# Full attention of 16 narrow heads with maxima made in advance: the last five units cut into two of 256 queries each, in place of the last one only

## The reference, cut to what matters

```
q = _rope(proj(Wq, bq)); k = _rope(proj(Wk, bk)); v = proj(Wv, bv)
scores = jnp.einsum('bhqd,bhkd->bhqk', q, k) / jnp.sqrt(HEAD_DIM)
attn = jax.nn.softmax(scores, axis=-1)
ctx = jnp.einsum('bhqk,bhkd->bhqd', attn, v)
...
scores = jnp.einsum('bhqd,bhkd->bhqk', q, k) / np.float32(np.sqrt(hd))
scores = scores * scale[..., None]
aw = jax.nn.softmax(scores, axis=-1)
out = jnp.einsum('bhqk,bhkd->bhqd', aw, v).transpose(0, 2, 1, 3).reshape(b, s, d)
```

## Time and profile before

| | before |
|---|---|
| time, median of 3 runs | 3846.15 us (3838.41 to 3847.82) |
| time of the profiled execution | 3843.74 us |
| span of the profiled execution | 3841.9 us |
| PE busy | 3509.3 us, 91% of the span |
| DVE busy | 3039.8 us, 79% |
| ACT busy | 2333.1 us, 61% |
| POOL busy | 155.4 us, 4% |
| score products of maxima, line 1987 | 3712, mean 398 ns |
| maxima on DVE, line 2095 | 3456, 2108.3 us |
| exponentials, line 2053 | 1856, 1854.7 us |
| value products, line 2029 | 13824, mean 384 ns |
| granted TensorE clock, mean | 0.928 |

### The profile page before, as it was taken

One profiled execution on the slowest core, in us unless ns is written; L12 is line 12 of the kernel. 1 busy time (PEld: TensorE's weight loads), 2 busy tenths in 40 slices (PEclk: granted clock), 3 DMA queues, 4 the chain that ended last, 5 costly groups with the idle time before them and its releaser, 6 DMA issues.

```text
span 3841.9 us, 72549 instructions
## 1 busy us (share of the span) xinstructions
PE 3509.3 (91%) x29391; PEld 1433.7 (37%) x29391; DVE 3039.8 (79%) x6567; ACT 2333.1 (61%) x2742; POOL 155.4 (4%) x417
## 2 busy tenths in 40 slices
PE   5989899889999997899999989599997999999988
PEld 3766766612222224222222245222224222222264
DVE  5255755689999974899999837698974999999557
ACT  2222342238888884388888852257784488888832
POOL 0000000110000000100000000200001000000000
PEclk8889999969999998699999989689998799999989
DMA  0010210130000001300000000400002100000000
GB/s 29 1 45 1 53 32 1 29 99 21 2 2 2 2 2 33 99 2 2 2 2 2 2 23 1 121 2 2 2 2 73 50 2 2 2 2 2 3 22 12
DMA packets 32116, 75.94 MB, mean 20 GB/s; under 512 B 10370, under 2 KB 25542, under 8 KB 26406
## 3 DMA queue, kind: packets, MB, share of 16 engines
q1 hardware_dynamic: 31638, 69.64, 6.3%
q10 hardware_dynamic: 144, 1.66, 0.1%
HBM read 56.54 MB, written 14.73 MB: 19 GB/s over the span
## 4 chain that ended last, share of the span: by engine, by line
PE 48%; DVE 43%; ACT 4%; issue 2%; SPq 2%; POOL 1%; DMA 1%; ACTq 0%; DVEq 0%
DVE pm L2095 36%; PE ps L2029 9%; PE ps L1987 6%; PE ps L966 4%; PE ps L2010 3%; PE ps L969 3%; PE ps L2311 3%; PE ps L1046 3%; PE ps L2332 2%; ACT arena L2053 2%; PE ps L1269 2%; SPq L1406 1%; PE ps L765 1%; PE ps L2026 1%; PE ps L1646 1%
## 5 line engine op out<-in xcount | busy, mean ns | idle before, releaser
L2095 DVE TENSOR_REDUCE pm<-ps 128x1 f32<-128x512 f32 x3456 | 2108.3, 680 | 92.6 <-PE ps L1987 87.1
L2053 ACT ACTIVATE arena<-ps 128x1024 f32<-128x1024 f32 (+1 forms) x1856 | 1854.7, 1001 | 438.1 <-PE ps L2010 310.0
L1987 PE MATMUL ps<-arena 64*128 64x512 bf16 (+1 forms) x3712 | 1303.3, 398 | 55.8 <-DMA arena<-parts_dram 43.2
L2029 PE MATMUL ps<-arena,VA 128*16 128x256 f32 (+1 forms) x13824 | 1079.7, 384 | 29.1 <-ACT EV L2074 24.2
L2010 PE MATMUL ps<-arena 64*128 64x512 bf16 (+1 forms) x3520 | 1017.0, 379 | 8.7 <-DMA arena<-m_dram 8.0
L1987 PEld LDWEIGHTS ps<-arena 64*128 64x128 bf16 x3712 | 329.6, 93 | 1110.3 <-DVE pm L2095 859.1
L2029 PEld LDWEIGHTS ps<-arena,VA 128*16 128x16 f32 x13824 | 228.1, 94 | 505.9 <-ACT arena L2053 400.0
L2010 PEld LDWEIGHTS ps<-arena 64*128 64x128 bf16 x3520 | 186.5, 94 | 64.3 <-issue 49.0
L985 ACT ACTIVATE EV<-ps 128x512 f32<-128x512 f32 x128 | 76.3, 598 | 203.3 <-PE ps L966 203.3
L997 DVE TENSOR_TENSOR arena<-EV,ps 128x512 f32<-128x512 f32 x128 | 87.7, 685 | 120.9 <-PE ps L969 115.4
L966 PE MATMUL ps<-XNT,arena 128*128 128x512 f32 x304 | 161.4, 613 | 2.3 <-DVE arena L1325 1.5
(11 more groups left out here) (280 smaller groups left out, 2831.0 us busy)
## 6 DMA issues: line engine op xcount, KB each, us to landing
arena<-parts_dram SPq DMA_DIRECT2D x192, 128.0 KB, 2.9
parts_dram<-parts SPq DMA_DIRECT2D x32, 384.0 KB, 2.9
arena<-in_pad SPq DMA_DIRECT2D x16, 512.0 KB, 7.6
arena<-k_dram SPq DMA_DIRECT2D x20, 268.0 KB, 4.2
arena<-in_w SPq DMA_DIRECT2D x4, 1024.0 KB, 5.8
parts<-k_dram SPq DMA_DIRECT2D x8, 268.0 KB, 3.9
arena<-in_w12T SPq DMA_DIRECT2D x1, 2048.0 KB, 9.5
arena<-m_dram SPq DMA_DIRECT2D x122, 6.0 KB
```

Of the source, the lines that this page charges most:

```text
L1987: ins = e.matmul(bank[:, 0:w], QR[half(par), q, 2 * g + pp, qt * P:(qt + 1) * P], KT[half(par), kc, 2 * g + pp, 0:w], start=True, stop=True)
L2029: ins = e.matmul(c.bank(4)[32 * hh:32 * hh + VW, a:b], c.VA[:, j, GH * g + hh, :], self.PB[:, (first + hh) % self.PBS, a:b], start=j == 0 ...
L2053: e.activation(self.PB[:, s:s + 2, offs[0]:CH], c.bank(t % 4, 2).rearrange("p (a t) -> p a t", a=2)[:, :, offs[0]:CH], ACT.Exp, scale=self ...
L2095: e.tensor_reduce(top, bank, AX, ALU.max).then_inc(self.emptied_v.sem, 1)
```

## The change: five units cut in two

The class gets a constant HALVED = 5, and in a full stage the last five units (11 to 15), not the last one alone, are replaced by two each, of the first and of the last 256 queries. They are called 11a, 11b and so on here. The units of the causal stage stay as they are.

```
-    LEAD, EARLY, AHEAD = 9, 4, 14
+    LEAD, EARLY, AHEAD, HALVED = 9, 4, 14, 5
...
         else:
-            g, k, _, _ = self.units.pop()
-            self.units += [(g, k, 0, TPC // 2), (g, k, TPC // 2, TPC)]
+            last = self.units[-self.HALVED:]
+            self.units[-self.HALVED:] = [(g, k, a, a + TPC // 2) for g, k, _, _ in last for a in (0, TPC // 2)]
```

## The result

The change makes the kernel slower, by less than half of what was forecast:

| | before | after |
|---|---|---|
| time, median of 10 runs | 3845.89 us (3838.41 to 3851.34) | 3854.01 us (3848.41 to 3856.86) |
| ratio, 95% interval | | 1.0020 (1.0012 to 1.0028) |
| span of the profiled execution | 3841.9 us | 3851.8 us |
| DVE busy | 3039.8 us | 3048.2 us |
| PE busy | 3509.3 us | 3514.4 us |

What follows compares the result with a forecast made beforehand. VectorE's reductions bound the kernel, with TensorE just fitting under; after the change both bind. Three full stages at +7.0 us give +21 us on the profiled 3843.74, 3864.7; forecast 3865 us, range 3851 to 3884.

Steps and rivals of the forecast that it cites:

- step 1: Score products in ticks of two maxima: four narrow ones idle half of TensorE's rows, +0.11 us, a tick of 1.20 us.
- step 3: TensorE's sum over half units in a full stage: both engines bind, 0.9 us per half unit, 7.0 us a stage.
- step 2: More unit ends on VectorE: four added joins, "rows" and outputs raise its floor by 3.4 us a stage (2.5 to 4.0).
- The low bound: In ticks of two maxima: the third score product overtakes the second, so narrow products add 0 us; dropped for program order.
- Step 3's low end: Lowest total for a full stage with both engines at their bound: 4.8 us, in a range to 10.2.
- The price of a matmul by itself: Two more score products a tick on TensorE: 25 ns each by the skill's page, put at nothing.
- Step 4: GpSimd's 5 operations and SyncE's 3 DMAs for each added unit, and ScalarE's 8 more tile copies, cost nothing.
- Rival A: TensorE doesn't bind in two-maxima ticks; only VectorE's floor is left: +10 us, 3854 (3851 to 3856); chance 0.26.
- Rival B: Narrow score products cost more than columns: ticks of 1.31 us, 3899, or 3882 with half of that; chance 0.10.
- Rival C: Stretches behind the second and third full stage run at TensorE's full clock: 22 us saved, 3832, faster; chance 0.03.

## Why the prediction was wrong

The direction and the bound were right: VectorE's reductions set the pace at 0.598 us each, and a full stage pays for each added unit end. What was wrong is the size: 7.0 us a stage were forecast and 2.5 measured. Of the 4.5 too much, 3.6 come from step 1 and what step 3 built on it, and 0.9 from step 2.

- **Step 1, "if the third, on the free half, can't overtake it, that half idles"; I took +0.11 us a tick. It failed.** It can. The trace of the change shows the second maximum starting before a score product that is ahead of it, the tick with narrow products alone is 1.09 us as before, and the reversed parities cost nothing. I said that rows of before couldn't tell, which is so, and chose the middle by the rule of the Trainium skill, TensorE: Matmul & The Clock Gate, on what overlaps with packed tiles (matmuls start and end in program order). This trace disagrees with it: 1303.51 before 1303.61. The low bound should not have fallen away on it, when the rows showed that products wait but not in which order they start.
- **Step 3, "both are at their bound in every tick", fell with it.** Where TensorE catches up, its ticks stayed at 1.09 to 1.18 us, so it kept the slack with which it works off copies and transposes. VectorE got no gaps: between 1217 and 1400 us it waited 0.6 us in all for products of line 1987, and 1.2 us before the change. The 0.9 us a half unit was 0.31 (20.01 - 19.70).
- **Step 2, VectorE's floor, was the right sum, mis-sized.** I had +3.4 us a stage, measured +2.5. Join and "rows" are 0.52 together, not 0.62, since I took the output step from the starts of its two instructions (0.51) and it costs 0.62 to 0.64. A half-width one is 0.37, put at 0.4, so that splitting an output step adds 0.12 and three add under 0.4, where 0.9 was taken.
- **Step 3's low end**, 4.8 us a stage, doesn't follow from its terms, which give 6.5 x 0.7 + 0.6 + 0.5 = 5.65.
- **The price of a matmul by itself** was put at nothing, and the ticks of 1.09 us with two more products bear that out. The Trainium skill, TensorEngine Tiling (Array Packing), on instruction overhead, has about 60 cycles for each; this trace doesn't show them as an addition.
- **Step 4 was right.** The chains by GpSimd and SyncE, four more a stage, cost no more than this: the half units keep 20.01 us to a hundredth.
- **Rival A** was the case, by its mechanism (overtaking) and nearly by its time: 3854 stood there and 3854.01 was measured. That the numbers meet to 0.01 us is luck: it added 10 us to an execution 2.15 us under the median, and the rise was 8.1. I gave it 0.26. **Rival B** is out by the narrow products alone. **Rival C** did not occur: the 34.1 us that lie as far behind the last join of the second and third full stage show a clock of 0.51 and 0.53, with TensorE busy for 22 and 23 of them.

## What to carry to other kernels

Where an engine runs without gaps, a change is worth what it adds to that engine's stream, and the distance between two recurring marks (here the joins) gives that to 0.01 us where whole runs scatter by 10. It misses what lies outside the marks, as the first units with the later join show. Cutting work into more units costs the bound engine each unit's own end, even if all columns stay the same; an instruction that reads the result of the one just before it also waits for that one's end, and putting one independent instruction between them took 0.12 us off each unit here (the whole program got 5 to 13 us faster). And a question that the trace of before can't answer should be kept open in the range, not settled by a rule.

## What the runs showed of the hardware

Products on the two 64-row halves of TensorE go on independently of program order, at least past one that waits: in ticks with two maxima a product of 512 columns on one half started 0.10 us before a score product for the other half that stands ahead of it. Four products of 256 columns in place of two of 512 cost nothing that shows (a tick of 1.09 us either way). On VectorE a reduction of 128x512 from PSUM shows 0.68 us but follows the last one after 0.598; a join of 128x64 to 128x16 between two costs 0.25 us where it waits for the last one's end (0.85 between their starts), and about 0.10 where it doesn't (0.70).
